# The end of the last stage of two transformer layers: where the experts' rows are read back and merged, and by which engine

## The reference, cut to what matters

```
xn = _layernorm(x, axis=-1)
x = x + _L1_attn_ref(xn, ...) + _L1_ffn_ref(xn, ...)

# inside _L1_ffn_ref: 8 experts, each token takes its best two
combine = jnp.zeros((T, E), x.dtype).at[jnp.arange(T)[:, None], sel].set(rw)
for e in range(E):
    g = jax.nn.silu(x @ w_gate[e]) * (x @ w_up[e])
    y = g @ w_down[e]
    out = out + combine[:, e:e + 1] * y
```

## Time and profile before

| | us |
|---|---|
| median of 3 runs | 1091.43 |
| lowest and highest of them | 1089.68, 1092.42 |
| the profiled execution's own time | 1091.52 |
| its span, first to last instruction | 1089.6 |
| the last expert block's store issued by GpSimd, from | 1063.1 |
| SP's eight loads issued, from | 1065.5 |
| residual of chunk 15 on VectorE, from | 1072.5 |
| merging of the four batches on VectorE | 1073.0 to 1086.2 |

### The profile page before, as it was taken

How to read it: one execution, slowest core, us unless ns; L and a number is a source line. 1 busy time by engine, 2 the same in 40 slices (tenths; PEclk the granted TensorE clock), 3 DMA queues, 4 the chain that set the end, 5 groups by cost and what they waited for, 6 DMA issues and landing times. The chain is left out here.

```text
span 1089.6 us, 16172 instructions
## 1 busy us (share of the span) xinstructions
PE 946.9 (87%) x5323; PEld 614.9 (56%) x5323; DVE 588.4 (54%) x1218; ACT 433.1 (40%) x663; POOL 314.5 (29%) x218
## 2 busy tenths in 40 slices
PE   3789999999858999998999988575999999999991
PEld 2678888888711234453445445463666666666660
DVE  4556655563268767647755741474443443443435
ACT  3335536353234554674576467041222222222220
POOL 3632515225233000211021020143333433433321
PEclk9999999999957989888998988786999999999995
DMA  5622414033051221133233112628873433433316
GB/s 200 217 96 60 165 58 144 19 97 126 1 166 58 92 79 60 59 107 131 92 101 118 55 59 99 161 106 298 241 234 86 122 104 88 118 106 97 98 43 236
DMA packets 149836, 125.26 MB, mean 115 GB/s; under 512 B 63232, under 2 KB 127504, under 8 KB 149776
## 3 DMA queue, kind: packets, MB, share of 16 engines
q1 hardware_dynamic: 146032, 114.25, 33.9%
q0 software_dynamic: 3744, 10.23, 2.7%
HBM read 85.56 MB, written 38.86 MB: 114 GB/s over the span
## 5 line engine op out<-in xcount | busy, mean ns | idle before, releaser
L1180 DVE TENSOR_REDUCE b_negmax<-b_psM 128x1 f32<-128x512 f32 x256 | 163.2, 683 | 82.1 <-PE b_psM L1408 79.1
L1090 ACT ACTIVATE b_probs<-b_psE 128x512 f32<-128x512 f32 x256 | 138.8, 595 | 122.8 <-PE b_psE L1426 121.8
L1408 PE MATMUL b_psM<-b_kst,b_qst 96*128 96x512 bf16 x256 | 98.9, 433 | 27.9 <-DVE b_negmax L1180 14.0
L1426 PE MATMUL b_psE<-b_qst,b_kst 98*128 98x512 bf16 x256 | 90.0, 412 | 15.1 <-ACT b_probs L1090 10.5
L402 POOL TENSOR_TENSOR a_hh<-a_h,a_hh 128x512 fp32r<-128x512 f32 x44 | 57.8, 1313 | 144.7 <-ACT a_hh L455 144.7
L1426 PEld LDWEIGHTS b_psE<-b_qst,b_kst 98*128 98x128 bf16 x256 | 21.0, 100 | 109.6 <-ACT b_probs L1090 54.1
L1435 PE MATMUL b_psV<-b_probs,b_vst 128*32 128x512 f32 x512 | 75.9, 667 | 3.1 <-ACT b_probs L1090 3.1
L1928 PE MATMUL d_psG<-d_w,d_xT 128*128 x156 | 76.5, 614 | 2.2 <-DVE d_xT L1827 1.9
L1776 POOL DMA_INDIRECT scratch_ys<-d_y,put x39 | 39.7, 1017 | 129.2 <-ACT d_y L1808 127.8
L1953 PE MATMUL d_psY<-d_w,d_hidden 128*128 x312 | 74.9, 383 | 0.0
L1936 PE MATMUL d_psU<-d_w,d_xT 128*128 x156 | 74.5, 600 | 0.0
(11 more groups left out here) (314 smaller groups left out, 2125.5 us busy)
## 6 DMA issues: line engine op xcount, KB each, us to landing
scratch_parts<-a_part SPq DMA_DIRECT2D x12, 512.0 KB, 4.3
b_qst<-scratch_parts SPq DMA_DIRECT2D x96, 64.0 KB, 2.1
b_kst<-scratch_parts SPq DMA_DIRECT2D x96, 64.0 KB, 2.1
scratch_parts<-b_part SPq DMA_DIRECT2D x24, 256.0 KB, 3.4
chunk_qst<-scratch_parts SPq DMA_DIRECT2D x96, 64.0 KB, 2.9
chunk_kst<-scratch_parts SPq DMA_DIRECT2D x96, 64.0 KB, 2.2
a_cbc<-scratch_cT SPq DMA_DIRECT2D x16, 256.0 KB, 3.9
scratch_v<-a_v SPq DMA_DIRECT2D x4, 1024.0 KB, 4.4
```

Source lines behind the costliest of these rows:

```text
L1090: nc.scalar.activation(probs[k % PSLOTS][:, h, :], psE[h % 2][:, :], ACT.Exp, scale=float(HD) ** -0.5).then_inc(scores_used[h % 2], 1)
L1180: nc.vector.tensor_reduce(negmax[i][:, t, h:h + 1], psM[:, h % 2, :], AX_X, ALU.max, negate=True).then_inc(rows_used[h % 2], 1)
L1408: nc.tensor.matmul(psM[:, h % 2, :], qst[g][0:STACK, h, t * P:(t + 1) * P], kst[g][0:STACK, h, :], start=True, stop=True).then_inc(rows_re ...
L1426: nc.tensor.matmul(psE[h % 2][:, :], kst[g][0:STACKM, h, k * P:(k + 1) * P], qst[g][0:STACKM, h, :], start=True, stop=True).then_inc(score ...
```

## The change

Four things are changed behind the last expert block.

1. The eight loads are split: SP issues the four of batches 0 and 1, ScalarE the four of batches 2 and 3. ScalarE's stand behind its whole walk, with the same waits for the blocks' stores.
2. VectorE merges batch 0 (its eight instructions, after waits for the batch's rows and residuals) at the head of step 7 of chunk 15, that is ahead of line 1870 of that chunk. Batches 2 and 3 it merges behind its walk, as before.
3. GpSimd merges batch 1, behind its own walk, in four tensor_tensor instructions of 128x1024: the first rows times their weights, in place, added to `xacc`; then the second rows times theirs, added.
4. SP waits for the batches in the order 0, 2, 1, 3 and stores each.

The two semaphores that count halves and wholes become one of each for every batch, and GpSimd gets one of its own. Nothing else is changed.

```diff
+        def load_back(eng, b):
+            for i in range(2):
+                eng.dma_start(w[:, b, i * TILES * D:(i + 1) * TILES * D].rearrange("p (t d) -> p t d", d=D),
+                              scratch["ys1"][i * TOK + b * SEQ:i * TOK + (b + 1) * SEQ, :]
+                              .rearrange("(t p) d -> p t d", p=P)).then_inc(back_in[b], 16)
...
         def _(sp):
...
-            for b in range(BATCHES):
-                for i in range(2):
-                    sp.dma_start(w[:, b, i * TILES * D:(i + 1) * TILES * D].rearrange("p (t d) -> p t d", d=D),
-                                 scratch["ys1"][i * TOK + b * SEQ:i * TOK + (b + 1) * SEQ, :]
-                                 .rearrange("(t p) d -> p t d", p=P)).then_inc(back_in[b], 16)
-            for b in range(BATCHES):
-                sp.wait_ge(added, b + 1)
+            for b in (0, 1):
+                load_back(sp, b)
+            for b in (0, 2, 1, 3):
+                sp.wait_ge(added[b], 1)
                 sp.dma_start(out[b * SEQ:(b + 1) * SEQ, :].rearrange("(t p) d -> p t d", p=P),
                              xacc[:, b * TILES:(b + 1) * TILES, :]).then_inc(stored, 16)
...
         def _(pool):
...
             walk({"light": light, "turn": turn, "down": down})
+            pool.wait_ge(o_done, 2 * TILES)
+            pool.wait_ge(back_in[1], 32)
+            x = xacc[:, TILES:2 * TILES, :]
+            for i in range(2):
+                rows = w[:, 1, i * TILES * D:(i + 1) * TILES * D].rearrange("p (t d) -> p t d", d=D)
+                nc.gpsimd.tensor_tensor(rows, rows, wts[i][:, TILES:2 * TILES].unsqueeze(2).to_broadcast((P, TILES, D)),
+                                        ALU.mult).then_inc(weighted, 1)
+                pool.wait_ge(weighted, i + 1)
+                if i:
+                    pool.wait_ge(half_added[1], 1)
+                nc.gpsimd.tensor_tensor(x, rows, x, ALU.add).then_inc(added[1] if i else half_added[1], 1)
...
         def _(act):
...
             walk({"light": light, "gate": gate, "turn_h": turn_h, "down": down})
+            for s in range(YSLOTS):
+                act.wait_ge(put_out[s], 16 * ((BLOCKS - 1 - s) // YSLOTS + 1))
+            for b in (2, 3):
+                load_back(act, b)
...
         def _(dve):
...
+            def merge_batch(b):
+                dve.wait_ge(back_in[b], 32)
+                dve.wait_ge(o_done, min((b + 1) * TILES, CHUNKS))
+                for i, done in enumerate((half_added[b], added[b])):
+                    if i:
+                        dve.wait_ge(half_added[b], 1)
+                    for t in range(TILES):
+                        n = b * TILES + t
+                        last = nc.vector.scalar_tensor_tensor(xacc[:, n, :], w[:, b, (i * TILES + t) * D:(i * TILES + t + 1) * D],
+                                                              wts[i][:, n:n + 1], xacc[:, n, :], ALU.mult, ALU.add)
+                    last.then_inc(done, 1)
...
             def normalise(n):
+                if n == CHUNKS - 1:
+                    merge_batch(0)
                 dve.wait_ge(rs_done, n + 1)
...
-            dve.wait_ge(o_done, CHUNKS)
-            for b in range(BATCHES):
-                dve.wait_ge(back_in[b], 32)
-                for i in range(2):
-                    if i:
-                        dve.wait_ge(half_added, b + 1)
-                    for t in range(TILES):
-                        n = b * TILES + t
-                        last = nc.vector.scalar_tensor_tensor(xacc[:, n, :], w[:, b, (i * TILES + t) * D:(i * TILES + t + 1) * D],
-                                                              wts[i][:, n:n + 1], xacc[:, n, :], ALU.mult, ALU.add)
-                    last.then_inc(added if i else half_added, 1)
+            merge_batch(2)
+            merge_batch(3)
```

More of the change, by code:

```diff
@@ L1701, in layer1_main @@
             sem(n) for n in ("scaled", "normed", "normT_ps", "normT", "o_ps", "o"))
-        back_in, half_added, added, stored = sems("back_in", BATCHES), sem("half_added"), sem("added"), sem("stored")
+        back_in, half_added, added = (sems(n, BATCHES) for n in ("back_in", "half_added", "added"))
+        weighted, stored = sem("weighted"), sem("stored")
         CHUNK_IN = 16 * CHUNK_LOADS
```

## The result

The changed kernel takes 1099.69 us (median of 6 runs, 1096.52 to 1101.11) against 1091.93 us of the kernel before in the same runs: 1.0068 times as long, 95% interval 1.0047 to 1.0089. The profiled execution took 1096.52 us, with a span of 1094.7 us.

What follows compares the result with a forecast made beforehand. VectorE's 13.26 us of merging behind the residual was taken as the bound. Delays of 5.68 + 6.5 = 12.2 us and late batch 2 rows put the span 8.1 us later: 1091.52 + 8.1 = 1099.6 us, range 1094.5 to 1101.5.

Steps and rivals of the forecast that it cites:

- Batch 0 ahead of the normalisation: Chunk 15's scaling (L1870) queues behind batch 0's landing and eight merges on VectorE, starting 5.68 us later.
- Three turns: GpSimd's multiply, add, multiply each hold up VectorE, after the seventh merge, the eighth and L1870: 6.5 us; chance 0.45.
- ScalarE's loads: Loads of batches 2 and 3 issue only after the last transpose's copy (L1818); batch 2 lands 5.2 us later.
- VectorE's wait for batch 2: Behind the residual VectorE idles from 1085.1 to 1087.75 for rows that used to be there.
- The sum: Whole end of kernel: last merge ends at 1094.3, span at 1097.7 against 1089.6, 8.1 us more.
- the flow that stops at 1079.7: Before the change, the loads' flow stops at about 1079.7, so loads don't bound the merging stage.
- No exclusion: Rival: merges keep 0.41 us beside GpSimd, only late loads cost; +1.6, 1093.1 us; chance 0.12.
- a port kept by VectorE: Rival: VectorE goes ahead of waiting GpSimd through L1870 and L1874; +4.3, 1095.8 us; chance 0.18, shared with one turn.
- Two turns: Rival: GpSimd asks 0.2 us later, finds the eighth merge under way, loses one multiply; +5.9, 1097.4 us; chance 0.22.
- The order of the stores: At the kernel's end, waiting for batches in the order 0, 2, 1, 3 before storing costs nothing.

Runs made afterwards that it cites:

- x1: Changed kernel with batch 1 merged by VectorE behind the residual, GpSimd merging nothing, stores in order 0 to 3; 1.0025 times the kernel before.
- x3: Changed kernel with all eight loads on SP in the order of batches, none on ScalarE; 1.0045 times the kernel before.
- y1: Kernel before, plus four GpSimd adds of 128x1024 on tiles nobody uses, from batch 1's landing on; tail 32.2 us.
- x5: x1 with all loads on SP and batch 0 merged between the last chunk's normalisation and the residual; 0.9992 times the kernel before.
- z1: x5 with a semaphore for each load, half batches merged as rows land, last store in two halves; 0.9981 times the kernel before.
- y2: Kernel before, plus eight GpSimd fills of 128x1024 with zeros on tiles nobody uses, from batch 1's landing on; tail 24.1 us.

## Why the prediction was right

- **Batch 0 ahead of the normalisation** was put at 5.68 us, and it is 5.68 in x1, where nothing else disturbs it.
- **Three turns**: the count and the places are those predicted (after the seventh merge, the eighth, L1870), in the changed kernel and in x3. The size was off: 6.5 us forecast, 5.4 measured (14.71 less 9.33). The multiply by weights was taken from a row with another broadcast, 2.36 us, and takes 1.89 alone; the add was taken at 2.13, from a row of subtractions (L1050), and takes 2.34. Multiply, add, multiply are 6.1, not 6.85, and each waiting VectorE instruction saved (6.1 - 5.4) / 3 = 0.24 us rather than 0.13.
- **ScalarE's loads** were put behind the end of L1818's copy. The first is issued 0.08 us behind the copy's start, 0.3 us sooner than assumed: the copy was still under way, and nothing in ScalarE's queue waits for its end. Batch 2 lands 1079.96 + 4.71 - 1079.54 = 5.1 us behind the first issue, where 5.2 was forecast.
- **VectorE's wait for batch 2** is 2.27 us; the forecast has it from 1085.1 to 1087.75, so 2.65 us.
- **The sum**: +8.1 us forecast for the tail, +6.7 measured; the difference of 1.4 is 1.1 for the turns and 0.4 for the wait, less 0.1 because the last sixteen merges take 6.67 us instead of 6.57. That the forecast time, 1099.6, is met within 0.1 us is therefore partly chance: the timed difference is 7.4 us with 2.3 either way, and it stands on a median of before of 1091.93 us rather than on the 1091.52 of the sum. The mechanism and its steps are shown; the last microsecond is not.
- **A reading that was off**: the flow that stops at 1079.7 is not that of the loads alone. The last load is issued at 1071.1 and lands 7.8 us later, at 1078.9; what flows behind it is batch 0's store, issued at 1076.39. No term of the sum rests on it.
- **The rivals.** No exclusion (+1.6) is ruled out by the three turns and by y1, a port kept by VectorE (+4.3) by the three turns. Two turns (+5.9) is ruled out by the count in the trace alone: by its size the measured +6.7 lies nearer to it than to the forecast's +8.1, and the margin of time on which the third turn hangs was, as the prediction says, small. Of the parts of the change none that was taken out gained: without GpSimd's part the tail is 26.3 us (x1), without ScalarE's 28.4 (x3), and with batch 0 behind the normalisation and neither of them, 22.1 (x5). The order of the stores was not changed alone, but from the end of the last merge to the end of the span it is 1094.7 - 1091.37 = 3.33 us in the changed kernel, against 3.36 before. GpSimd's part together with batch 0 behind the normalisation was not run.

## What to carry to other kernels

Work that is put ahead of a step of a chain costs the chain its whole length and the wait for its data, less what the step would have waited anyway (here 8.45 us less 2.77); the same work behind that step can fill the idle time which the chain leaves. Before a second engine is given part of some elementwise work, look in the trace for instructions of both at the same time: GpSimd and VectorE on SBUF operands took turns here, and each GpSimd instruction that overlapped cost VectorE 1.6 to 2.1 us. Three such turns cost 5.4 us, where the whole batch that GpSimd took over is 3.3 us of work on VectorE. And a DMA issued from another engine's queue starts when that queue gets to it, here with the last copy.

## What was not expected

The time ahead of the tail varies far more than the tail: the first load of experts' rows is issued between 1060.0 and 1069.3 us in ten profiled executions, of code that is the same up to there. It goes roughly with TensorE's mean granted clock; what sets that clock was not looked into. Spans and clocks of z1 and of x1:

```profile
core 0: 1083.0 us, clock 0.924
```

```profile
core 0: 1095.1 us, clock 0.912
```

Of the 12.1 us between these two spans, 6.0 are tail and 6.1 lie ahead of it (1068.81 against 1062.71). The tail itself repeats: in y2, where nothing disturbs the merges, it is 24.1 us as before, though its first load comes 3.8 us later. And in all seven kernels that were timed beside the one before, the difference of the tails lies within the interval of the timed runs. So a change of 2 to 4 us at the end of this kernel can be read from one tail, while twelve timed runs of z1 left it uncertain by 1.9 us either way.
